# Gated cross-attention block on one core: four PSUM banks for the five linear layers, transposes into banks that are free at the time, and the padding of the queries moved to ScalarE

## The reference, cut to what matters

```python
def xattn(q, k, v):                     # B = 4, S = 512, D = 512, H = 16 heads of HD = 32
    Q = (q @ Wq.T + bq).reshape(bs, sl, H, HD)
    K = (k @ Wk.T + bk).reshape(bs, sl, H, HD)
    V = (v @ Wv.T + bv).reshape(bs, sl, H, HD)
    score = einsum('bshd,bsgd->bshg', Q, K)      # heads attend to heads of the same token
    weight = softmax(score, axis=-1)
    attn = einsum('bshg,bsgd->bshd', weight, V).reshape(bs, sl, nf)
    return attn @ Wo.T + bo

x = x + tanh(g_xattn[0]) * xattn(layernorm(x), ctx_2048, ctx_2048)
x = x + tanh(g_ffn[0]) * (layernorm(x) @ (weight * scale_weight[:, None]).T + bias)
```

## Time and profile before

| | |
|---|---|
| median of 3 runs | 311.43 us (308.17 to 313.33) |
| profiled execution, its own time | 311.65 us |
| its span, first to last instruction | 309.9 us |
| outside the span (311.65 less 309.9) | 1.75 us |
| mean granted TensorE clock | 0.96 of full speed |
| busy: PE, DVE, ACT, POOL | 276.1, 226.8, 127.8, 119.5 us |

### The profile page before, as it was taken

The page is one execution under the profiler, slowest core; times in us unless marked ns, Lnnn a source line. Parts: engine busy times, 40 slices in busy tenths (PEclk is TensorE's granted clock), DMA queues, the critical chain, the costliest instruction groups (busy, mean ns, idle before and its releaser), DMA issues.

```text
span 309.9 us, 7795 instructions
## 1 busy us (share of the span) xinstructions
PE 276.1 (89%) x3124; PEld 220.8 (71%) x3124; DVE 226.8 (73%) x364; ACT 127.8 (41%) x243; POOL 119.5 (39%) x126
## 2 busy tenths in 40 slices
PE   7989995599794599999989999999996999799696
PEld 6868874477673388787868777777775878686585
DVE  3769999569544499579974897489947694698673
ACT  5554344650536202852168204931286006636310
POOL 3143319712255015831382236531583015211732
PEclk9999999689998989999999999999999999899699
DMA  6938881500407640572226530763037102423002
GB/s 229 391 93 268 181 268 71 112 26 0 137 30 242 139 137 4 169 170 98 104 72 203 130 135 0 262 144 135 0 115 184 43 0 70 106 33 122 17 35 102
DMA packets 57830, 37.03 MB, mean 119 GB/s; under 512 B 35920, under 2 KB 45392, under 8 KB 57808
## 3 DMA queue, kind: packets, MB, share of 16 engines
q1 hardware_dynamic: 57808, 36.73, 39.4%
HBM read 25.71 MB, written 11.01 MB: 118 GB/s over the span
## 4 chain that ended last, share of the span: by engine, by line
DVE 25%; DMA 20%; PE 17%; issue 12%; POOL 9%; ACT 8%; SPq 8%; DVEq 0%; POOLq 0%; ACTq 0%
PE acc L463 11%; DMA v_scratch<-v_or_norm 6%; DMA x_scratch<-raw_spare 4%; DMA out<-late 4%; ACT late L775 4%; DVE stats L914 4%; PE score_ps L463 4%; SPq L362 3%; DMA x_spare<-wf_t 3%; POOL rstd L1266 3%; POOL shift L1271 3%; DVE late L1086 2%; DVE spread L1055 2%; DVE k_t L974 2%; SPq L347 2%
## 5 line engine op out<-in xcount | busy, mean ns | idle before, releaser
L463 PE MATMUL acc<-wo_parts,xa_parts 128*128 128x512 f32 x168 | 46.6, 436 | 9.4 <-ACT xa_parts L692 6.8
L1266 POOL TENSOR_TENSOR rstd<-var_eps,minus_half 128x1 f32<-128x1 f32 (+1 forms) x24 | 21.5, 895 | 83.7 <-DVE var_eps L925 83.7
L463 PEld LDWEIGHTS acc<-wo_parts,xa_parts 128*128 128x128 f32 x168 | 34.7, 211 | 18.7 <-issue 4.6
L463 PE MATMUL acc<-wk_parts,ctx_parts 128*128 128x512 f32 x144 | 38.9, 426 | 6.5 <-DVE late L1086 4.1
L775 ACT ACTIVATE late<-attn_ps 32x256 f32<-32x256 f32 x112 | 42.1, 376 | 2.6
L748 ACT ACTIVATE v_or_norm<-late,shift,rstd 128x512 f32<-128x512 f32 x12 | 9.8, 814 | 76.2 <-POOL shift L1271 76.2
L463 PEld LDWEIGHTS acc<-wk_parts,ctx_parts 128*128 128x128 f32 x144 | 28.8, 206 | 15.7 <-issue 5.7
L463 PE MATMUL acc<-wv_parts,ctx_parts 128*128 128x512 f32 x144 | 34.7, 395 | 0.0
L463 PE MATMUL acc<-wq_parts,xa_parts 128*128 128x512 f32 x144 | 33.9, 391 | 0.1
L463 PE MATMUL acc<-wf_parts,x_parts 128*128 128x512 f32 (+1 forms) x132 | 30.1, 383 | 1.9 <-DVE v_or_norm L967 1.9
L463 PEld LDWEIGHTS acc<-wq_parts,xa_parts 128*128 128x128 f32 x144 | 26.7, 188 | 6.2 <-DVE k_t L974 0.4
(11 more groups left out here) (112 smaller groups left out, 465.6 us busy)
## 6 DMA issues: line engine op xcount, KB each, us to landing
x_norm<-x SPq DMA_DIRECT2D x8, 512.0 KB, 3.9
v_scratch<-v_or_norm SPq DMA_DIRECT2D x8, 512.0 KB, 3.2
v_keys<-v_scratch SPq DMA_DIRECT2D x16, 256.0 KB, 3.7
x_res<-x SPq DMA_DIRECT2D x8, 512.0 KB, 3.3
ctx_raw<-ctx_t SPq DMA_DIRECT2D x7, 512.0 KB, 4.5
out<-late SPq DMA_DIRECT2D x13, 256.0 KB, 2.7
x_scratch<-raw_spare SPq DMA_DIRECT2D x5, 512.0 KB, 3.1
raw_spare<-x_scratch SPq DMA_DIRECT2D x20, 128.0 KB, 2.6
```

Source lines behind the costliest of these rows:

```text
L463: last = pe.matmul(dst, left(a, k), right(b, k), start=(n == 0), stop=(n == len(terms) - 1))
L1266: nc.gpsimd.tensor_tensor(rstd[which][:, t], var_eps[which][:, t], minus_half[:, t], ALU.pow).then_inc(n_rstd[which], count)
```

## The change

The layers get four banks, `acc[0..3]`; the two banks `turn_ps` are gone. A function `bank(layer, chunk, t)` says which pair a layer writes: in the middle chunks q, o and f use `acc[t]`, k and v use `acc[2+t]`, with exceptions for the first and last chunks. x1 of chunks 0, 1, 2 is transposed into `score_ps`, `attn_ps` and `acc[2+t]`, x2 into `score_ps` (chunk 5 into `acc[t]`). The waits follow: o still for f's residual, k for `v_bias` of the chunk before, q for o's residual, v for `k_turn`, f for `q_turn`, `turn_x2` for the transposed scores, and `score` for the low part of x2.

The queries: `q_bias` becomes one DVE addition of the bias in place on `q_t`, and ACT makes the two padded copies (`q_pads`, two ACTIVATEs of 128x1024 with a per-partition scale), ahead of `attn_copy`. Chunk 1 keeps the two DVE instructions.

Orders change too. SP loads `scale_row` and the feed-forward weights ahead of `load_x(1)`. POOL does `scale_w` before `ctx_low(2)`, and `root(0, i+2)` before `root(1, i-1)`. ACT does `exp(0)` and the high parts of the feed-forward weights ahead of its first step, and in the loop `x1_apply(i+2)` ahead of `x2_apply(i-1)`. DVE takes the first statistics of chunk i+2 before `spread_first(i)` and the `second_stats` earlier, in step 1 the statistics of chunk 3 before the low part of x2. Step 6 of every engine takes the order of the middle steps (o first). In step 7 PE runs attend(7) before the second f tile of chunk 5.

```diff
-        acc = [psum(f"acc{i}") for i in range(2)]
-        turn_ps = [psum(f"turn_ps{i}") for i in range(2)]
+        acc = [psum(f"acc{i}") for i in range(2 * TILES)]
...
+        def bank(layer, c, t):
+            even = acc[t][:], acc[TILES + t][:]
+            if layer == "v":
+                return attn_ps[:, BANK * t:BANK * (t + 1)] if first(c) else even[1]
+            if layer == "k":
+                return even[0 if second(c) else 1]
+            if layer == "q":
+                return even[1 if second(c) else 0]
+            if layer == "o":
+                return even[1 if isinstance(c, int) and c >= CHUNKS - 2 else 0]
+            return even[0]
+        def x1_bank(c, t):
+            return (score_ps[t][:], attn_ps[:, BANK * t:BANK * (t + 1)], acc[TILES + t][:])[c]
+        def x2_bank(c, t):
+            return acc[t][:] if late_f(c) else score_ps[t][:]
... sync
+            sp.dma_start(scale_row[:], scale.partition_broadcast(P)).then_inc(scale_in, DMA)
+            for j in range(2):
+                load_w(WF, j)
             load_x(1)
... tensor, loop step
-                    o_layer(i - 1, "f", i - 2)
-                    k_layer(i + 1, "o", i - 1)
-                    q_layer(i + 1)
+                o_layer(i - 1)
+                k_layer(i + 1)
+                q_layer(i + 1)
                 attend(i)
+                if late_f(i - 1):
+                    v_layer(i + 1, tiles=(0,))
+                    turn_x2(i - 1)
+                    return v_layer(i + 1, tiles=(1,))
+                turn_x2(i - 1)
+                v_layer(i + 1)
+                f_layer(i - 1)
... tensor, step 7
                     o_layer(i - 1, "v", i, (1,))
+                    attend(i)
+                    turn_x2(i - 1, (0,))
                     late_f_tile(i - 2, 1)
-                    turn_x2(i - 1, x2_read(i - 2), (0,))
-                    attend(i)
... scalar
+            def q_pads(c):
+                act.wait_ge(q_biased, 1 if first(c) else c)
+                reached(act, score_mm, 2 * c)
+                for slot in range(PAD):
+                    nc.scalar.activation(q_pad[:, slot], q_t[:], ACT.Identity, scale=own_slot[:, slot:slot + 1]
+                                         ).then_inc(q_padded, 1)
... scalar, loop step
+                exp(i)
+                x1_high(i + 1)
+                if exists(i + 2):
+                    x1_apply(i + 2)
                 x2_apply(i - 1, 0)
                 x2_apply(i - 1, 1)
...
                     x2_high(i - 1)
-                    attn_copy(i, (0, 1))
-                    attn_copy(i, (2, 3))
+                    q_pads(i + 1)
+                    attn_copy(i)
... vector
             def q_bias(c):
+                dve.wait_ge(q_turned, TILES * (c + 1))
+                nc.vector.tensor_tensor(q_t[:], q_t[:], bq_heads[:].unsqueeze(3).broadcast_to([P, QH, KC, GT]),
+                                        ALU.add).then_inc(q_biased, 1)
... vector, loop step
-                turned_lo(xa_parts, x1_hi, x1_lo, i + 1, src=x1_source(i + 1))
+                x1_low(i + 1)
+                if exists(i + 2):
+                    norm_stats(0, x_norm, i + 2)
+                spread_first(i)
+                second_stats(i - 1, 0)
                 k_turn(i + 1, 0)
-                spread_first(i)
+                second_stats(i - 1, 1)
                 k_turn(i + 1, 1)
-                second_stats(i - 1, 0)
                 k_bias(i + 1)
                 q_turn(i + 1, 0)
-                second_stats(i - 1, 1)
-                if exists(i + 2):
-                    norm_stats(0, x_norm, i + 2)
                 q_turn(i + 1, 1)
                 q_bias(i + 1)
... gpsimd
             pool.wait_ge(scale_in, DMA)
             for j in range(2):
                 scale_w(j)
+            ctx_low(2)
             for j in range(2):
                 wf_low(j)
```

More of the change, by code:

```diff
@@ L692, in high, with turned_hi @@
                 return nc.scalar.activation(dst, src, ACT.Identity)
-            def turned_hi(parts, ready, done, c, free, tiles=range(TILES), src=turned_by_pe):
+            def turned_hi(parts, ready, done, c, free, src, tiles=range(TILES)):
                 for t in tiles:
@@ new lines, in _, with first_step @@
+            exp(0)
+            w_high(WF, 0)
+            w_high(WF, 1)
+            def first_step():
+                spread_some(0)
+                act.wait_ge(gates_done, 1)
+                act.wait_ge(consts_in, 2 * DMA)
+                for row, n in ((bo_row, 0), (bf_row, 1)):
+                    nc.scalar.activation(row[:], row[:], ACT.Identity, scale=tanh_g[:, n:n + 1]
+                                         ).then_inc(rows_scaled, 1)
+                attn_copy(0, (0,))
+                x1_apply(2)
+                attn_copy(0, (1,))
+                x1_high(2)
+                exp(1)
+                attn_copy(0, (2, 3))
+                attn_high(0, 0)
+                attn_high(0, 1)
@@ new lines, in second_step, with last_softmax_step @@
+            def second_step():
+                q_pads(2)
+                x2_apply(0, 0)
+                attn_copy(1, (0,))
+                x2_apply(0, 1)
+                x2_high(0)
+                x1_apply(3)
+                attn_copy(1, (1, 2, 3))
+                attn_high(1, 0)
+                attn_high(1, 1)
+                ctx_high(3)
+            def last_softmax_step(i):
+                exp(i)
+                spread_some(i)
+                x2_apply(i - 1, 0)
+                last_attn_copy(i, 0)
+                x2_high(i - 1, (0,))
+                attn_high(i, 0)
+                x2_apply(i - 1, 1)
+                last_attn_copy(i, 1)
+                attn_high(i, 1)
+                x2_high(i - 1, (1,))
@@ L901, in low, with turned_lo @@
                 return nc.vector.tensor_tensor(dst, src, hi.bitcast(F32), ALU.subtract)
-            def turned_lo(parts, hi_done, done, c, tiles=range(TILES), src=turned_by_pe):
+            def turned_lo(parts, hi_done, done, c, src, tiles=range(TILES)):
                 for t in tiles:
@@ L1359, in pool_step @@
                     spread_last(i)
+                if exists(i + 2) and not first(i - 1):
+                    root(0, i + 2)
                 if exists(i - 1):
@@ L1362, in pool_step @@
                     root(1, i - 1, 1, 1)
[L1363 to L1364 removed]
+                if first(i - 1):
+                    root(0, 3)
                 if exists(i - 1):
```

403 lines of the change are left out of this document (170 added, 233 removed).

## The result

| | before | after |
|---|---|---|
| median of 4 runs each | 312.38 us (308.17 to 314.74) | 296.38 us (294.04 to 297.67) |
| ratio, 95% interval | | 0.956 [0.942, 0.969] |
| profiled execution; span | 311.65; 309.9 us | 295.94; 293.3 us |

A forecast was written before the change was run, and what follows sets the result against it. PE bounds the loop at its own rate; elsewhere it waits, partly at a slow clock. 46.5 + 36.7 + 36.0 + 99.2 + 27.3 + 41.6 = 287.3 us, plus 1.75 outside the span: 289 us, range 283 to 300.

The forecast's parts named there:

- the first rival: Whole kernel: the removed waits come back elsewhere, such as q(3) waiting the full 4 us and slowing; 300 us, chance 25%.
- a sign of being wrong: Listed signs: PE waiting for x1 of chunk 1, o(i) waiting in each loop step, or step 2 over 39 us.
- step 2: Step 2, 43.37 us before: waits at o(1) and k(3) go, q(3) takes over 2.9 us; 36.0 us (33.6 to 40).
- the start: Start and step 0, 46.08 us before: chain to score(0) grows by 0.4 us net; 46.5 us (46 to 48).
- step 6: Step 6, 28.60 us before: with o first, k(7)'s wait of 2.37 us goes; 27.3 us (27 to 28.6).
- the tail: Steps 7 and 8, 45.99 us before: o(6)'s wait stays, the last attention's 2.61 us goes; 41.6 us (40 to 45).
- the sentence that costs the weights' move at nothing: Start and step 0: loading 1.25 MB earlier fits a stretch with transfers 0.15 busy, so it costs nothing.
- Steps 3 to 5: Loop, 100.65 us before: 0.48 us per step to give, no more; 3 x 33.07 = 99.2 us (98.8 to 101).
- its thinnest cover: Loop: x1's low part ends 12.3 us into the step, q(i+1) can start at 13.0, a cover of 0.7 us.
- Step 1: Step 1, 45.21 us before: the 5.04 us wait for x1 of chunk 2 goes; 36.7 us (35.3 to 39).
- the stop in score(1): Step 1: PE loses 1.4 us inside score(1) with no releaser; kept in the sum.
- a slow tile of o(6): Step 7: o(6) still waits 1.85 us and loses 1.7 us to slow clock (4.59 against 2.87).

The follow-up runs named there:

- run 7: Kernel after, with scale row and feed-forward weights loaded, scaled and split at their old places: span 301.3 us against 293.3, step 1 41.24 us.
- run 8: Padded queries made by DVE again in every chunk, on top of run 3: loop steps of 32.6 us, span 293.0 us.
- run 5: Kernel after, with the feed-forward weights' low part not computed (POOL writes zeros at its start): score(1) 3.4 us earlier, step 1 35.59 us, span 294.8 us.
- run 2: Kernel after, with SP in step 1 saving chunk 0's output before loading chunk 2's values: step 2 35.45 us, 4.9 less; span 291.8 us.
- run 3: Kernel after, with DVE in the loop taking both attention low parts before the second feed-forward residual: steps 32.10, 32.09, 32.06 us; span 291.7 us.
- run 9: Run 6 with POOL's two low parts of the feed-forward weights moved into gaps: 286.4 us, ratio 0.916. A second way, four pieces in place, has no total.
- run 6: Kernel after with the edits of run 2 and run 3 together: span 284.6 us, profiled again 285.5; timed 287.5 us, ratio 0.926.

## Why the prediction was right, and where its terms were off

**Right.** The direction, the range, and which waits would go. Still, 296.4 lies above the forecast's own bounds of 285 to 294, which had 68%: part of the first rival came true, q(3) with its full wait and a slow layer, and so did a sign of being wrong, a step 2 over 39 us. Four stages left their bounds: the start and step 2 were too long, step 6 and the tail too short, so the total is nearer than its terms. Of the removed waits, run 7 shows the biggest, at x1 of chunk 2, to be due to the weights' move; that the new orders took away those of step 6 and of the tail is read from the rows, and no run tried it alone.

q(3) took over step 2's wait, ended by x1's low part, from the chain on SP. Of the earlier trace rows, k(7) no longer waits, and the tail's wait of 2.61 us is gone; o(1) still waits 1.54 us, where none was expected. The pads cost 1.144 us each (forecast 1.13), DVE's addition 1.225 (1.25), where the earlier trace rows had only relatives. Against the pads on ACT the prediction had weighed the Trainium skill's page "ScalarE: Activation LUTs", section "Rules for kernel authors", by which VectorE should multiply; run 8 has them back on DVE and loses 0.5 us a loop step.

**The start and step 0, 46.5 against 51.23.** The failing step is the sentence that costs the weights' move at nothing. It weighed only transfers, and those did fit. What the move brought along was POOL's work on the weights, now inside step 0's softmax. By run 5 that is 3.2 us. The rest is score(0), 1.9 later than before. PE's own list came 0.7 later to it in this execution, a difference that the start shows between executions of one kernel too; and score(0) waited 1.13 us for the pads on ACT, where before it had waited for nothing. Behind that wait lie two more meetings of DVE and POOL: `k_bias(0)` took 2.23 instead of 1.21 us beside POOL's low part of context 1, and POOL's second `shift` for x1 of chunk 1 took 1.30 instead of 0.26 us beside DVE's new addition, so that ACT came to the pads 0.9 us after that addition was done. What each is worth was not tried.

The trace of before had such a meeting, in step 1, so it could have been foreseen:

```profile
48.02 2.46 POOL L1284 TENSOR_TENSOR wf_raw<-wf_raw,scale_row 128x1024 f32<-128x1024 f32 x1
48.04 2.47 DVE L925 TENSOR_SCALAR var_eps<-moments 128x2 f32<-128x2 f32 x1
```

The same `TENSOR_SCALAR` takes 0.17 us elsewhere.

**Step 2, 36.0 against 40.36.** The wait at q(3) was taken as 2.9 from 0.5 to 4; it was 5.37, the slow layer cost 1.6 more, and o(1) waited 1.54. The chain on SP was as long as the text had it: 17.8 us from `x1_apply(3)` to `o_residual(1)` (82.95 to 100.72), against 17.5. What was mis-sized is where it begins and what follows: `x1_apply(3)` came 4.1 us before score(2), not 6, and from the residual to q(3) it took 6.0 us, not 4.5 to 5.5. The text counted the save behind the load of values in SP's list as given; run 2 shows that this order alone held 4.9 us.

**Steps 3 to 5, 99.2 against 100.16: close, by two errors.** A step with no more than 0.34 us of waiting takes 32.1 us, not 33.07: the durations that were added overlap at their ends (24 matmuls are listed with 5.73 us, but the next group starts 5.44 to 5.6 later). So the loop had some 1.4 us per step to give, not 0.48 "no more", and with the low parts first it gave them (run 3). Against that, two steps paid 1.9 us for a meeting of DVE and POOL that the text did not see; a third of it came at q, where the text had named its thinnest cover, 0.7 us. Before, POOL came 0.4 us behind DVE at all four such turns. That one step of three escaped it is luck.

**Step 1 (36.7, 35.83), step 6 (27.3, 26.05), tail (41.6, 39.67).** Each a little better, in part from the same overlap. In step 1 the 1.4 us that were kept for the stop in score(1) vanished behind a wait, not by the change; in their place the first tile of k behind that wait took 4.25 instead of 2.87 us, at a granted clock of 0.69. In the tail, 1.6 us are luck: the text kept a slow tile of o(6), and in this execution it ran in 3.04 us behind a wait of 2.31. Where it took 4.6 us, the tail is 41.3 to 42.1, as forecast.

The Trainium skill, page "SBUF — State Buffer", section "Who interferes with whom", has the rule that the prediction missed: a DVE instruction with two inputs in SBUF contends with a GpSimd instruction that reads SBUF, and whichever comes second waits until the first is done. The traces agree: 2.9 against 0.69 us at the turns, POOL's 2.95 against 2.42 where the two start within 0.02 us and POOL is the one to wait (by the recorded times it is 0.01 us ahead there, which tells no order), and 2.84 against 5.06 us in pieces. The same section counts `tensor_scalar` among the operations that can take both ports; the 0.77 against 0.17 us of run 9 agree.

## What to carry to other kernels

Moving a load earlier moves everything that consumes it: list the consumers' engines and check what each will run beside, VectorE beside GpSimd above all. When the start order of two such instructions hangs on some hundredths of a microsecond, take them apart by order (run 3) rather than hope, and read a gain of one stage from that stage's length, since the span of a single run carries the luck of the others. Banks that free an order are priced together with it: here the new order without them lost 6 us a step, and the banks without the new order were not tried.

## What was not expected of the hardware

- A start earlier by 0.03 us decided between 34.1 and 32.1 us for a whole loop step.
- A VectorE instruction of 128x2 was held 0.6 us by GpSimd in run 9, and 2.3 us in the kernel before.
- TensorE stops for 0.9 to 1.4 us at a fixed place in its program (five traces), and where it waits 2.3 us or more just ahead of that place, the stop is not seen.
- Behind like waits of 2.3 us the same tile of the same kernel (run 6) ran in 3.0 us at a granted clock of 1.00, and in 4.6 us at 0.63 when that kernel was profiled again.
